# Moving a softmax sum to another PSUM bank, and two residual adds to a later place in the vector queue

## The reference

```python
def attn(x, w_qkva, gamma):            # w_qkva: 3072 x 1024
    h = rmsnorm(x, gamma)
    q, kv, a = split(h @ w_qkva.T, 3)
    a = sigmoid(a)
    y = scan over positions: y[t] = a[t] * y[t-1] + kv[t]
    return q * y

def ffn(x, W1, b1, W2, b2, Wg, bg):    # 8 experts, hidden size 128
    gate = softmax(x @ Wg + bg)        # over the 8 experts
    h = relu(x @ W1[e] + b1[e])
    y = h @ W2[e] + b2[e]
    return sum over e of gate[e] * y[e]

x = x + attn(layernorm(x), ...)
x = x + ffn(layernorm(x), ...)
```

## Time and profile before

| what | value |
|---|---|
| median of 2 runs | 547.49 us (538.97 and 556.01) |
| the profiled execution's own time | 542.28 us |
| span of its slowest core (core 5) | 540.7 us, mean granted TensorE clock 0.867 |
| spans of the eight cores | 534.3, 529.9, 521.7, 535.3, 533.4, 540.7, 522.4, 533.6 us |
| TensorE matmul (PE) busy | 415.7 us, 77% of the span |
| VectorE (DVE) busy | 237.3 us, 44% |
| ScalarE (ACT) busy | 114.0 us, 21% |
| GpSimd (POOL) busy | 102.0 us, 19% |
| moved by the DMA engines | 32.06 MB, 59 GB/s on average |

### The profile page before, as it was taken

The page is one execution under the profiler, slowest core; times in us unless marked ns, Lnnn a source line. Parts: engine busy times, 40 slices in busy tenths (PEclk is TensorE's granted clock), DMA queues, the critical chain, the costliest instruction groups (busy, mean ns, idle before and its releaser), DMA issues.

```text
span 540.7 us, 4763 instructions; the slowest of 8 cores (521.7 to 540.7 us)
## 1 busy us (share of the span) xinstructions
PE 415.7 (77%) x1540; PEld 150.8 (28%) x1540; DVE 237.3 (44%) x356; ACT 114.0 (21%) x179; POOL 102.0 (19%) x76
## 2 busy tenths in 40 slices
PE   1335399825899998596889998596889998867994
PEld 0102144301223443122223442122323442222331
DVE  0463433345376443545175443464365443762321
ACT  2120010540222115300223116200232106202200
POOL 5000011404600124037000114045000123230000
PEclk9956698976779999958989998867979999979888
DMA  7999992090000000900400001900300000003003
GB/s 119 219 166 157 163 165 44 2 227 5 0 1 1 1 1 6 227 1 1 156 0 1 1 1 44 190 0 1 155 0 2 0 1 1 1 0 155 2 0 155
DMA packets 18231, 32.06 MB, mean 59 GB/s; under 512 B 656, under 2 KB 4752, under 8 KB 18208
## 3 DMA queue, kind: packets, MB, share of 16 engines
q0 software_dynamic: 9584, 14.98, 18.1%
q1 hardware_dynamic: 8624, 16.79, 9.9%
HBM read 38.35 MB, written 8.39 MB: 86 GB/s over the span
## 4 chain that ended last, share of the span: by engine, by line
PE 59%; DMA 17%; DVE 13%; issue 4%; ACT 2%; another core or an unknown queue 2%; POOL 1%; DVEq 0%; ACTq 0%; POOLq 0%
PE ps_kv L414 11%; PE ps_a L433 10%; DMA xbf<-xT 9%; PE ps_q L482 9%; PE ps_kv L720 8%; DMA wq_bf<-wqT 7%; PE ps_a L827 6%; PE ps_kv L827 3%; PE ps_a L720 3%; DVE rows L235 2%; PE ps_q L288 2%; DVE rows L657 2%; PE ps_rep L770 1%; DVE wq_bf L199 1%
## 5 line engine op out<-in xcount | busy, mean ns | idle before, releaser
L505 POOL TENSOR_TENSOR x_sb<-x_sb,y_sb 128x512 f32<-128x512 f32 x32 | 40.5, 1264 | 287.1 <-DVE y_sb L493 287.0
L414 PE MATMUL ps_kv<-hbf,wq_bf 128*128 128x512 bf16 x256 | 68.2, 396 | 18.0 <-DVE carry L460 8.8
L433 PE MATMUL ps_a<-hbf,wq_bf 128*128 128x512 bf16 x256 | 63.4, 392 | 5.1 <-DVE wq_bf L199 5.1
L482 PE MATMUL ps_q<-hbf,wq_bf 128*128 128x512 bf16 x256 | 60.1, 383 | 0.0
L456 DVE TENSOR_TENSOR_SCAN y_sb<-asig,carry,ps_kv 128x512 f32<-128x512 f32 x24 | 30.7, 1280 | 62.6 <-ACT asig L445 62.6
L445 ACT ACTIVATE asig<-ps_a 128x512 f32<-128x512 f32 x32 | 19.1, 597 | 161.5 <-PE ps_a L433 161.5
L720 PE MATMUL ps_kv<-hbf,w_bf 128*128 128x512 bf16 x192 | 48.1, 404 | 3.2 <-DVE x_sb L841 3.2
L288 PE MATMUL ps_q<-xbf,statc 128*1 128x512 bf16 x32 | 14.2, 617 | 38.8 <-DMA xbf<-xT 38.8
L414 PEld LDWEIGHTS ps_kv<-hbf,wq_bf 128*128 128x128 bf16 x256 | 25.5, 100 | 56.8 <-issue 33.3
L827 PE MATMUL ps_a<-h1g,w_bf 128*128 128x512 bf16 x128 | 39.5, 465 | 0.0
L433 PEld LDWEIGHTS ps_a<-hbf,wq_bf 128*128 128x128 bf16 x256 | 25.5, 101 | 37.6 <-issue 11.6
(11 more groups left out here) (82 smaller groups left out, 392.1 us busy)
## 6 DMA issues: line engine op xcount, KB each, us to landing
x_sb<-xT SPq DMA_DIRECT2D x4, 2048.0 KB, 14.6
outT<-x_sb SPq DMA_DIRECT2D x4, 2048.0 KB, 6.6
wq_bf<-wqT POOLq DMA_DIRECT2D x3, 2048.0 KB, 40.6
xbf<-xT POOLq DMA_DIRECT2D x3, 1024.0 KB, 17.4
w_bf<-w1p POOLq DMA_DIRECT2D x1, 2048.0 KB, 65.9
w_bf<-w2p POOLq DMA_DIRECT2D x1, 2048.0 KB, 77.2
xbf<-xT POOLq DMA_DIRECT2D x2, 512.0 KB, 11.9
wg_bf<-wgp POOLq DMA_DIRECT2D x1, 256.0 KB, 77.1
```

The costliest lines, as they stand in the source:

```text
L414: ii = tensor.matmul(ps_kv[:, j % 2, :], wq_bf[:, k, (8 + j) * 128:(9 + j) * 128], hbf[:, k, :], start=(k == 0), stop=(k == KC - 1))
L433: ii = tensor.matmul(ps_a[:, j % 2, :], wq_bf[:, k, (16 + j) * 128:(17 + j) * 128], hbf[:, k, :], start=(k == 0), stop=(k == KC - 1))
L482: ii = tensor.matmul(ps_q[:, j % 2, :], wq_bf[:, k, j * 128:(j + 1) * 128], hbf[:, k, :], start=(k == 0), stop=(k == KC - 1))
L505: ii = gpsimd.tensor_tensor(x2buf(c)[:, j, :], x_sb[:, j, :], y_sb[:, j, :], ALU.add)
```

## The change

There are two edits. The first puts the sum of the exponentials into `ps_q[0:1, 1]` instead of `ps_a[0:1, 0]`, and moves the waits for its reader: `emitY2grp` no longer waits for `dve_invs` before group 6, `emitE1` no longer waits for it before `e == 4`, and `emitS2` of the next chunk, which writes the same bank of `ps_q`, now waits for the `dve_invs` of the chunk before. The second takes the residual adds of groups 2 and 3 out of the pairs of `emitLn2` and puts them behind all five pairs. On TensorE the order of instructions is the same as before.

```diff
@@ emitS2
                 if c != 0:
                     tensor.wait_ge(s_gp.h, K["gp_sq"])
+                    tensor.wait_ge(s_dve.h, ck[c - 1]["dve_invs"])
@@ emitLn2
-        def emitLn2(c, outs_c=None):
+        def emitLn2(c):
...
                 rec_i(K["ln2k"], k, s_dve)
-                if outs_c is not None and k in (1, 3):
-                    emitOuts(outs_c, [2 if k == 1 else 3])
@@ emitSum
-                ii = tensor.matmul(ps_a[0:1, 0, :], ones_bf[0:8, 0:1], exg[:],
+                ii = tensor.matmul(ps_q[0:1, 1, :], ones_bf[0:8, 0:1], exg[:],
                                    start=True, stop=True)
@@ emitSumInv
-                ii = vector.reciprocal(row(R_GI), ps_a[0:1, 0, :])
+                ii = vector.reciprocal(row(R_GI), ps_q[0:1, 1, :])
@@ emitE1
                     if e == 4:
                         tensor.wait_ge(s_act.h, K["act_exp"])
-                        tensor.wait_ge(s_dve.h, K["dve_invs"])
@@ emitY2grp
-                    if d == 6 and next_c is not None:
-                        tensor.wait_ge(s_dve.h, ck[next_c]["dve_invs"])
@@ run_schedule
-                emitLn2(c, outs_c=(c - 1 if c > 0 else None))
+                emitLn2(c)
+                if c > 0:
+                    emitOuts(c - 1, [2, 3])
                 if c > 0:
                     emitY2grp(c - 1, [4, 5], c)
                     emitOuts(c - 1, [4, 5])
```

## The result

The changed kernel took 525.66 us (median of 11 runs, 519.32 to 529.99) against 539.82 us (median of 10 runs) for the kernel before. The ratio is 0.9687, with a 95% interval of 0.9637 to 0.9737. That is 16.9 us of 539.82, with an interval of 14.2 to 19.6; forecast were 17.14. The ratio is taken from the runs in the quicker of the chip's two states alone, so it is not the quotient of the two medians, and the profiled execution of the changed kernel, 529.18 us with a span of 527.6 on core 5, is not one of those runs. In e9's session the ratio came out at 0.967 (0.963 to 0.971).

The account below looks back on a forecast made before the run. TensorE was taken to set the pace, stalled by group 6's waits for the reciprocal and the slow clock after. 5.88 + 5.87 + 5.49 - 0.10 = 17.14 us off 542.28 gave 525.1 us, range 518 to 536.

Parts of the forecast that it names:

- The gap: Between the sum's end and group 6 on TensorE: the 3.69 us wait for the reciprocal goes in chunk 1.
- The clock of group 6: Group 6's eight matmuls stay at 2.4 GHz, taking 1.83 us instead of 3.52; clock gain 2.19 us in chunk 1.
- the first rival: Group 6 still runs at the low clock and keeps 3.52 us; only the waiting goes, 531.3 us; chance 0.10.
- Start of W1: First W1 matmul after group 7 comes earlier by 5.88, 5.87 and 5.49 us in chunks 1, 2 and 3.
- VectorE is what is late next: Adds of groups 6 and 7 queue behind the reciprocal, allowing W1 at 255.90; TensorE's 256.22 still decides, by 0.3 us.
- The moved waits: Fifth W1 group's wait goes, one comes before the next chunk's squares' sums; cost 0, at most 0.7 us.
- The two adds behind the norm: Adds 2 and 3, awaited by the scores, cost 0.10 us in chunk 3 only; bounds no gain and 1.8 us.
- the cover of 2.0 us: Before chunk 1's scores: adds 2 and 3 finish by 246.4, TensorE arrives at 247.84, so their cost is 0.
- the second rival: Low-clock stretches come back elsewhere, 5.1 us in all; only 12.0 us saved, 530.2 us; chance 0.13.
- No other signal of VectorE: Third rival: another VectorE signal holds group 6 or W1, so nothing is won, 542.3 us; chance 0.04.
- the level of chunk 0: Fourth rival: projections of chunks 1 to 3 slow to 2.10 us per group, 550.3 us; chance 0.03.

Follow-up runs that it names:

- e9: The changed kernel, unaltered, measured again in another session beside two variants; ratio to the kernel before 0.967 (0.9629 to 0.9711).
- e3: The changed kernel with group 6's wait for the reciprocal put back, the sum still in `ps_q`; ratio to the kernel before 1.0023.
- e2: The changed kernel with residual adds 2 and 3 back between the norm pairs, so only the sum's bank and waits differ from before; ratio 0.9656.
- e4: The kernel before with 16 unread matmuls between the sum and group 6, the wait kept; ratio 0.989.
- e1: The kernel before with only residual adds 2 and 3 moved behind the five norm pairs, sum and waits unchanged; ratio 1.0008.
- e5: The changed kernel with the gate's reciprocal done twice on VectorE, ahead of adds 6 and 7; ratio to the kernel before 0.9938.
- e4b: The kernel before with 8 unread matmuls between the sum and group 6, the wait kept; ratio 0.9967.
- e6: The changed kernel with the first W1 group waiting for residual add 5 instead of add 7; ratio to the kernel before 0.9587.

## Why the prediction was right

**The gap.** Forecast 3.69 us in each of three chunks. e3 brings it back as 3.70 with the wait alone, and e2 keeps the whole gain without the other edit. Shown.

**The clock of group 6.** Forecast 1.83 us instead of 3.52, since 0.91 us of idleness would not drop the level. It held in 24 of 24 chunks of the changed kernel, and e4 shows the cause by itself: with work in the gap the group is fast although it starts no earlier. The reason that I gave, that the level held for over half of today's gap, was an average over one window of one core, and e2 shows how near the edge it was. Taken together, with one profiled execution of each kernel:

| pauses of TensorE | at the low level behind them |
|---|---|
| before, e1, e3: 0.92 us ahead of the sum, then 3.70 us | group 6 in 72 of 72 |
| e5: 3.76 us ahead of W1 | W1 in 21 of 24 |
| e4b: 8 matmuls behind the sum, then 1.88 us | group 6 in 14 of 24 |
| e2: scores split by 0.31 to 0.67 us, then 0.92 us | group 6 in 5 of 14 |
| e4, e4b: the scores split in the same way, then 0.92 us | the filling matmuls in 2 of 26 |
| e2, e4, e4b: scores not split, then 0.92 us | 0 of 32 |
| changed kernel, e5, e6, e9: up to 0.79 us ahead of the scores, none inside, then 0.92 us | group 6 in 0 of 96 |

So the first rival (chance 0.10) was real. In the changed kernel the scores wait once for the add and then run without a break, and behind unbroken scores and the 0.92 us alone nothing was slow in any kernel. I take it that this order kept the rival away. It is a reading of the counts, and why seven of 40 split cases were slow and the others not, no run shows.

**Start of W1.** Forecast 5.88, 5.87 and 5.49 us earlier on core 5. Its sum to W1 fell from 11.61, 11.60 and 11.23 us to 5.72, 5.72 and 5.73, which is 5.89, 5.88 and 5.50.

**VectorE is what is late next.** Right in kind, with a size that was off: the slack is 0.5 us by e5, not 0.3. The adds start 3.28 us after the start of the reciprocal, where I had let 3.39 pass, and the two of them together take 1.21 us, not 1.30.

**The moved waits** cost nothing that the traces show: on no core does a wait at the squares' sums name the reciprocal.

**The two adds behind the norm.** This term was mis-sized. I had 0.10 us in chunk 3 and 0 elsewhere. Where the clock is at full in group 2, chunks 2 and 3 took between 12.93 and 13.11 us from the broadcast to the sum before, and between 13.31 and 13.61 after, 0.4 us more in most of them. In chunk 3 I had let the scores start 0.14 us after the add, and 0.24 were needed; and I compared 8 x 0.216 = 1.73 us without the last matmul's end (1.89 in the timeline) with an end that contained it. In chunk 2 the cover of 2.0 us came from slow groups 2 and 3 and is gone where they are fast. In chunk 1 it is gone too, as e1 shows, but there the wait for the add only takes the place of a pause of 0.67 us inside the scores, and the sum comes at 13.34 to 13.45 us where it came at 13.31 and 13.49. Where group 2 is slow it costs nothing (14.04 in chunk 3 in both). So it is up to 0.8 us in all, inside the bound of 1.8 us, and e1's ratio of 1.0008 does not resolve it.

**The other rivals.** Low-clock stretches did come back elsewhere on some cores (0.80 granted in one window above). W1 to the next projections took 27.64 us against 27.93 in the mean, so nothing was lost there. In this pair of executions 2.7 us were lost between the projections and the broadcast, 0.8 in e9's. So a part of the second rival (12.0 us saved) did happen in the profiled execution, whose saving was 542.28 - 529.18 = 13.1 us; the ratio over the runs does not show it. No other signal of VectorE held group 6. The projections of chunks 1 to 3 ran at 1.73 us per group as before, and the level of chunk 0 (2.10 us per group) appeared in none of them in any run.

**How near the number is.** That 16.9 us came out beside 17.14 is in part luck. The interval of the measurement is 5.4 us wide, the adds cost several times what I had given them, and the low-clock stretches that come and go move a core by more than the difference. What the traces bear out is the term of 17.1 us between the sum and W1. The 525.1 us also stand on a profiled execution of 542.28, 2.5 us above the later median of 539.82; from that median the same saving gives 522.7.

## What to carry to other kernels

A pause of TensorE can have two prices, the wait itself and the slow matmuls behind it; read both, the second from the granted clock and from the durations of the groups after the pause, on all cores. Before asking for a faster instruction, ask which tile the waiting one really needs: a one-row result in another bank freed 3.7 us of wait and 2 us of clock, three times. When a wait is gone, go on to the next pause on the same engine and put work that is ready into it; that took the ratio from 0.967 to 0.949.

## What was not expected

Added work that nobody reads made the kernel 1.1% faster (e4), and the same 1.88 us pause slowed the group behind it on one core and left it alone on another (e4b). With the adds between the norm pairs, a pause of 0.31 to 0.67 us inside the scores was at times enough for the group that came behind the next 0.92 us to be slow, in 5 of 14 cases of e2, while 0.79 us just ahead of the scores never was. So moving the adds has an effect on both sides: 0.4 us lost in a quick chunk, and a slow group of 1.65 us avoided in some. Which side weighs more the times do not tell: 0.9656 (0.9566 to 0.9747) with the adds between and 0.9687 (0.9637 to 0.9737) with them behind.
